# Layer 0's recurrence: GpSimd makes both tiles' gating products and the query products beside VectorE's four sums, and the first stage is put in another order

## The reference, cut to what matters

```python
def step(carry, xs):                       # 32 chunks, one after the other
    W_in, W_out = carry                    # each 4 x 8 per sequence and head
    q_t, k_t, v_t, lr_t = xs
    k_h = softmax(einsum('blhd,bDhd->blhD', k_t, W_in), -1) * lr_t[..., 1:]
    q_h = softmax(einsum('blhd,bDhd->blhD', q_t, W_in), -1)
    qk = einsum('bqhD,bkhD->bhqk', q_h, k_h) * mask
    o_t = einsum('bqhD,bDhd->bqhd', q_h, W_out) + einsum('bhqk,bkhd->bqhd', qk, v_t)
    W_out = W_out + einsum('bnhD,bnhd->bDhd', k_h, v_t)
    for _ in range(2):
        g_out, g_in = -attn(W_in, k_t, v_t), -attn(W_out, v_t, k_t)
        W_in, W_out = W_in - lr_in * g_in, W_out - lr_out * g_out
    return (W_in, W_out), o_t
...
# the experts: top 2 of 8 for each token
gate = silu(x @ wg.T); up = x @ wu.T; y = (gate * up) @ wd.T
```

## Time and profile before

| | |
|---|---|
| median of 3 runs | 1335.31 us |
| the profiled execution | 1332.25 us |
| its span, first to last instruction | 1330.5 us |
| VectorE busy | 1224.0 us (92%) |
| TensorE busy | 1002.1 us (75%), mean granted clock 0.873 |
| ScalarE busy | 718.4 us (54%) |
| GpSimd busy | 701.5 us (53%) |
| step 0 of the recurrence begins | 126.07 us |
| step 4, the first with experts, begins | 203.92 us |
| step 28 begins | 646.56 us |
| the last step, 31, begins | 710.05 us |

### The profile page before, as it was taken

One profiled execution on the slowest core, in us unless ns is written; L12 is line 12 of the kernel. 1 busy time (PEld: TensorE's weight loads), 2 busy tenths in 40 slices (PEclk: granted clock), 3 DMA queues, 4 the chain that ended last, 5 costly groups with the idle time before them and its releaser, 6 DMA issues. The chain is left out here.

```text
span 1330.5 us, 15940 instructions
## 1 busy us (share of the span) xinstructions
PE 1002.1 (75%) x3654; PEld 580.4 (44%) x3655; DVE 1224.0 (92%) x2277; ACT 718.4 (54%) x1364; POOL 701.5 (53%) x637
## 2 busy tenths in 40 slices
PE   3865347878878887787577576668899889898874
PEld 2522335555555555555445532233444444444431
DVE  7998799999999999999997779989999899989999
ACT  5654015555555555555334565457667666766741
POOL 5038732333333333333210017789789778878885
PEclk9687558889889889999877598789999899999988
DMA  9749141000000000000162124455445444543346
GB/s 304 217 115 310 58 134 41 21 20 22 21 24 18 24 16 21 24 18 18 52 204 64 32 103 129 143 141 176 159 152 182 162 140 172 163 156 139 137 150 191
DMA packets 106772, 145.49 MB, mean 109 GB/s; under 512 B 26348, under 2 KB 82425, under 8 KB 101857
## 3 DMA queue, kind: packets, MB, share of 16 engines
q1 hardware_dynamic: 90816, 114.51, 27.2%
q0 software_dynamic: 10240, 25.32, 5.9%
q10 hardware_dynamic: 5664, 5.11, 1.2%
HBM read 112.26 MB, written 39.04 MB: 114 GB/s over the span
## 5 line engine op out<-in xcount | busy, mean ns | idle before, releaser
L2126 DVE TENSOR_TENSOR ps<-ps,cv 128x512 f32<-128x512 f32 x256 | 162.4, 679 | 1.9 <-DMA cv<-bc_scr 1.9
L1160 PE MATMUL ps<-Q,ident 128*128 128x512 f32 x206 | 115.2, 649 | 24.2 <-DVE Q L2144 7.5
L985 PE MATMUL ps<-wd_a,xn 128*128 x576 | 93.9, 313 | 42.8 <-ACT xn L1374 42.8
L1392 ACT ACTIVATE x<-x 128x128 f32<-128x128 f32 (+1 forms) x127 | 32.2, 278 | 143.3 <-DVE x L1953 65.0
L782 POOL DMA_INDIRECT y_tok<-xnT,meta x72 | 72.7, 1010 | 61.6 <-ACT xnT L1380 48.9
L965 PE MATMUL ps<-wg_a,xnT 128*128 x144 | 90.9, 717 | 17.5 <-issue 11.2
L985 PEld LDWEIGHTS ps<-wd_a,xn 128*128 128x128 f32 x576 | 79.2, 213 | 56.8 <-issue 55.3
L995 PE MATMUL ps<-x,ident 128*128 128x64 f32 x512 | 73.7, 297 | 29.1 <-DMA wu_a<-in_wu_a 12.3
L760 POOL DMA_INDIRECT slots_x<-xn,sl_put x64 | 75.2, 1174 | 37.9 <-issue 18.9
L791 POOL TENSOR_TENSOR xn<-xn 128x512 f32<-128x512 f32 x24 | 30.3, 1264 | 120.7 <-DVE x L1947 111.0
L995 PEld LDWEIGHTS ps<-x,ident 128*128 128x128 f32 x512 | 73.0, 217 | 43.4 <-issue 33.4
(11 more groups left out here) (383 smaller groups left out, 3041.0 us busy)
## 6 DMA issues: line engine op xcount, KB each, us to landing
cv<-bc_scr SPq DMA_DIRECT2D x64, 512.0 KB
xn<-bc_scr SPq DMA_DIRECT2D x24, 1024.0 KB
O<-bc_scr SPq DMA_DIRECT2D x8, 1024.0 KB
slots_x<-O POOLq DMA_DIRECT2D x28, 260.0 KB, 5.6
qkv_scr<-wg_a SPq DMA_DIRECT2D x24, 256.0 KB
xnT<-slots_x SPq DMA_DIRECT2D x72, 64.0 KB
x<-in_x SPq DMA_DIRECT2D x8, 512.0 KB, 6.4
y_tok<-slots_x SPq DMA_DIRECT2D x2, 2048.0 KB, 13.8
```

Source lines behind the costliest of these rows:

```text
L985: m = pe.matmul(ps[:, 0, 0:D], hidT[:, k, f * P:(f + 1) * P], wd_a[:, bass.ds(off + f * D, D)], start=(f == 0), stop=(f == FC - 1))
L1160: pe.matmul(ps[:, 4, :], ident[:], yc_of(c, n), start=(n == 0), stop=(n == NS - 1)).then_inc(y0_used, 1)
L2126: tt(dBu(g), ps[:, 2 + g, :], b_rows[:, n % 4, :], ALU.mult).then_inc((inject0, b_used)[g], 1)
```

## The change

In the recurrence: GpSimd also makes the gating product of tile 1 (ScalarE copies its up product first), beside L1963; tile 0's stays beside L1949; the step's own query product now goes beside L1894, the output product beside L1978. VectorE keeps only tile 2's. TensorE makes `o_sums` at the end of a routed step. One semaphore, `sum_begins`, counts the first two large products of each step. In the first stage: the query norms go ahead of the last four value projections and start with each square; ScalarE squares the queries ahead of the values' silus; the second half of V is loaded in two pieces; the gate copies are spread around the learning rates; the gate projections use seven banks, so that they need not wait for copies; TensorE waits for the experts' weights in step 3 and not before step 0.

```diff
@@ heads_load: rows lo to hi, and SyncE's calls
-            heads_load(sp, 1, 2, V, v_in)
+            heads_load(sp, 4, 6, 2, V, v_in)
+            heads_load(sp, 6, 8, 2, V, v_in)
@@ GpSimd
             def q_product(c):
-                pool.wait_ge(p3_ready, c)
+                pool.wait_ge(sum_begins, 2 * c + 1)
                 pool.wait_ge(q_ps, c)
                 pq_of(pool, c).then_inc(pq_ready, 1)
             def o_product(c):
                 pool.wait_ge(qh_ready, c + 1)
                 pool.wait_ge(o_ps, c + 1)
+                pool.wait_ge(p3_ready, c + 1)
                 op_of(pool).then_inc(op_ready, 1)
-            q_product(FIRST)
...
-            def gated_first(c):
-                pool.wait_ge(gate_silu, (c - FIRST) * TPS + 1)
-                pool.wait_ge(up_copied, c - FIRST + 1)
-                pool.wait_ge(p2_ready, c + 1)
-                pool.tensor_tensor(hid[:, 0, :], th[:, 0, :], up0, ALU.mult).then_inc(hid0_ready, 1)
+            def gated(c, k):
+                pool.wait_ge(gate_silu, (c - FIRST) * TPS + k + 1)
+                pool.wait_ge(up_copied, (c - FIRST) * (TPS - 1) + k + 1)
+                if k:
+                    pool.wait_ge(qh_ready, c + 1)
+                else:
+                    pool.wait_ge(sum_begins, 2 * c + 2)
+                pool.tensor_tensor(hid[:, k, :], th[:, k, :], ups[:, k, :], ALU.mult).then_inc(hid_pool, 1)
             for c in range(FIRST, NCH - 1):
+                q_product(c)
+                if FIRST < c <= AFTER:
+                    y_scatter(c - 1, 1)
                 if c < AFTER:
-                    gated_first(c)
+                    gated(c, 0)
                 if FIRST < c <= AFTER:
-                    y_scatter(c - 1, TPS - 1)
+                    y_scatter(c - 1, 2)
+                if c < AFTER:
+                    gated(c, 1)
+                    y_scatter(c, 0)
                 o_product(c)
-                q_product(c + 1)
-                if c < AFTER:
-                    for k in range(TPS - 1):
-                        y_scatter(c, k)
+            q_product(NCH - 1)
@@ TensorE
             def norms(n, sq, bank):
-                pe.wait_ge(squared, 4 * n + 4)
                 for e in range(HD):
+                    if e % 2 == 0:
+                        pe.wait_ge(squared, 4 * n + e // 2 + 1)
...
+            pe.wait_ge(lr_copied, B)
+            norms(1, sq_q, 7)
             for b in range(4, B):
                 project(2 * B + b)
-            pe.wait_ge(lr_copied, B)
-            norms(1, sq_q, 7)
             for b in range(B):
                 pe.wait_ge(conv_done, NCU)
-                since(pe, gate_copied, b - 3)
+                if b == 4:
+                    pe.wait_ge(slots_ready, 1)
+                since(pe, gate_copied, b - 6)
...
-            pe.wait_ge(slots_ready, 1)
-            pe.wait_ge(we_loaded, 16 * 3)
@@ TensorE, step
                 q_sums(c, 4, HD)
+                if after and not here:
+                    o_sums(c)
                 for k in range(2):
...
-                    if k == 0:
+                    if k == 0 and not here and not after:
                         o_sums(c)
+                if here:
+                    o_sums(c)
             with pe.Fori(0, FIRST - 1) as c:
                 step(c, False)
+            pe.wait_ge(slots_ready, 1)
+            pe.wait_ge(we_loaded, 16 * 3)
@@ ScalarE
+            act.wait_ge(q_in, 32)
+            for k in range(4):
+                square(Q, sq_q, 2 * k)
+            silu(2 * B)
+            for b in range(1, B):
                 silu(2 * B + b)
-                if b < 4:
-                    tap(2 * B + b + 4)
-...
+                if b < 5:
+                    tap(2 * B + b + 3)
             act.preload_act_table(ACT.Sqrt)
             norm_roots(1, 7)
...
             act.preload_act_table(ACT.Exp)
+            act.wait_ge(lr_stored, 16)
+            for b in range(3):
+                gate(b)
             act.wait_ge(lr_in, 1)
...
+            for b in range(3, B - 1):
+                gate(b)
             act.preload_act_table(ACT.Exp)
-            act.wait_ge(v_in, 32)
+            gate(B - 1)
@@ ScalarE, step
-                if not start:
-                    o_copy(c - 1)
                 if before:
                     y(c - 1, 1)
                 if here:
                     xT(c, 2)
+                if not start:
+                    o_copy(c - 1)
                 if before:
                     hT(c - 1, 2)
+                if start:
+                    act.wait_ge(v_in, 48)
...
                 if here:
+                    up_copy(c, 1)
                     act.preload_act_table(ACT.Silu)
...
-                if after:
+                if after and here:
                     xT(c + 1, 0)
                 exp(EQ, rec_q, exp_q)
...
                 if here:
                     y(c, 0)
+                if after and not here:
+                    xT(c + 1, 0)
                 if after:
-                    up_copy(c + 1)
+                    up_copy(c + 1, 0)
                     xT(c + 1, 1)
@@ VectorE, step
-                tt(PP, bc(VC, 1, 2 * DI), bc(both(WO[:]), 2, CH), ALU.mult).then_inc(p2_ready, 1)
-                dve.wait_ge(p2_ready, c + 1)
+                tt(PP, bc(VC, 1, 2 * DI), bc(both(WO[:]), 2, CH), ALU.mult).then_inc(sum_begins, 1)
+                dve.wait_ge(sum_begins, c * 2 + 2)
...
                 q_softmax()
-                gated(1)
                 if late:
```

More of the change, by code:

```diff
@@ L201, in build, with gate_bank @@
         logit_bank, rank_bank = (0, 1), (1, 2)
+        def gate_bank(b):
+            return (2, 3, 4, 5, 0, 1, 6)[b % 7]
         ring = wg_a[:].rearrange("p (u t) -> p u t", t=L)
@@ L210, in build @@
         r = Region(xn_rows[:])
-        th, hid, up0 = r.take(TPS, F), r.take(TPS, F), r.take(F)
+        th, hid, ups = r.take(TPS, F), r.take(TPS, F), r.take(TPS - 1, F)
         hidT = th
@@ L548, in op_of, with heads_load @@
             return eng.tensor_tensor(OP, bc(EQ, 2, HD), CS.rearrange("p (D e) l -> p D e l", D=DI)[:, :, :, 1:CH + 1], ALU.mult)
-        def heads_load(eng, half, w, dst, done):
-            turn = 2 * (1, 0, 2).index(w) + half
-            for u in range(4):
-                eng.wait_ge(stored[4 * (turn % 2) + u], 16 * (turn // 2 + 1))
-            eng.dma_start(dst[half * 64:(half + 1) * 64, :, :],
-                          qkv_scr[w, 4 * half:4 * half + 4].rearrange("b (h e) t -> (b h) e t", h=H)).then_inc(done, 16)
+        def heads_load(eng, lo, hi, w, dst, done):
+            for b in range(lo, hi):
+                eng.wait_ge(stored[b], 16 * ((1, 0, 2).index(w) + 1))
+            eng.dma_start(dst[lo * H:hi * H, :, :],
+                          qkv_scr[w, lo:hi].rearrange("b (h e) t -> (b h) e t", h=H)).then_inc(done, 16)
         block = ctx.enter_context(nc.Block())
@@ L742, in _ @@
                                pad).then_inc(zeroed, 16)
[L744 to L747 removed]
+            heads_load(pool, 0, 4, 1, K, k_in)
+            heads_load(pool, 4, 8, 1, K, k_in)
+            heads_load(pool, 0, 4, 0, Q, q_in)
+            heads_load(pool, 4, 8, 0, Q, q_in)
             pool.wait_ge(zeroed, ZEROED)
@@ L1332, in _, with gate @@
                 lr_copy(b)
-            for b in range(B):
-                silu(2 * B + b)
-                if b < 4:
-                    tap(2 * B + b + 4)
-                k = b - 2
-                if 0 <= k < 4:
-                    if k == 0:
-                        act.wait_ge(q_in, 32)
-                    square(Q, sq_q, 2 * k)
+            act.wait_ge(q_in, 32)
[3 more added lines that the diff above has]
+            for b in range(1, B):
+                silu(2 * B + b)
+                if b < 5:
+                    tap(2 * B + b + 3)
             act.preload_act_table(ACT.Sqrt)
             norm_roots(1, 7)
+            def gate(b):
+                act.wait_ge(gate_ps, b + 1)
+                act.activation(gateT[:, b * L:(b + 1) * L], ps[:, gate_bank(b), :], ACT.Copy).then_inc(gate_copied, 1)
             act.preload_act_table(ACT.Exp)
+            act.wait_ge(lr_stored, 16)
+            for b in range(3):
+                gate(b)
             act.wait_ge(lr_in, 1)
@@ L1349, in _ @@
             act.activation(LR[:], LR[:], ACT.Ln, bias=1.0).then_inc(lr_log, 1)
-            act.wait_ge(lr_stored, 16)
-            for b in range(B):
-                act.wait_ge(gate_ps, b + 1)
-                act.activation(gateT[:, b * L:(b + 1) * L], ps[:, 2 + b % 4, :], ACT.Copy).then_inc(gate_copied, 1)
+            for b in range(3, B - 1):
+                gate(b)
             act.preload_act_table(ACT.Exp)
-            act.wait_ge(v_in, 32)
+            gate(B - 1)
             temper = HD ** -0.5
@@ L1892, in step @@
                 r_k = o.mark(dve.reciprocal(Z3K[:, j:], Z3K[:, j:]))
-                o.wait(g_3)
+                dve.wait_ge(sum_begins, c * 2 + 1)
```

(6 more changed lines are left out.)

31 lines of the change are left out of this document (14 added, 17 removed).

## The result

| | before | after |
|---|---|---|
| median of the first measurement, 10 runs each | 1335.2 us | 1330.6 us |
| ratio, 95% interval | | 0.9956 [0.9938, 0.9975] |
| the profiled execution | 1332.25 us | 1329.91 us |
| its span | 1330.5 us | 1328.2 us |
| step 0 begins | 126.07 | 118.30 |

The forecast was 1322.6 us in a range of 1313.0 to 1330.0. The kernel became faster, by 4.6 us where 12.7 were expected, and its median lies 0.6 us above the range. The last two rows say where to look: layer 0 is 11.2 us shorter, close to the forecast, and layer 1, whose code is the same, took 8.8 us longer.

A forecast was written before the change was run, and what follows sets the result against it. VectorE, busy 92% of the span, was taken to bound the kernel. The terms -11.7 + 2.3 + 2.5 - 15.1 + 6 + 3.3 = -12.7 us gave a median of 1322.6 us, range 1313.0 to 1330.0.

The forecast's parts named there:

- first stage to step 3: First stage of layer 0: VectorE's waits of 3.27, 2.64 and 5.75 us go, -11.7 us.
- step 3 into 4: Step 3 of layer 0: output sums ahead of the first tile's transpose make step 4 begin at 194.5, +2.3 us.
- tiles of steps 4, 5: Steps 4 and 5: the fourth tile's rows come late behind the clearings, +2.5 us, bounds 0 and 5.
- routed steps: 24 routed steps: without tile 1's product VectorE saves 0.63 us a step, -15.1 us.
- late steps: Routed steps behind stretches of lower clock: ScalarE comes late in 6 or 7 of them, 0.9 us each, +6 us.
- tail: End of layer 0: output products 3.3 us later delay TensorE's variance sums, +3.3 us, bounds 0.5 and 4.5.
- further on everything follows VectorE: Behind the last steps of layer 0: everything keeps pace with VectorE, no further gain or loss, 0 us.
- the rival of the lock: Routed steps: VectorE's L1967 waits 0.26 us each for GpSimd's product, 6.2 us in all, result 1328.8 us; chance 0.13.
- VectorE stays the only bound: Layer 0: ScalarE's reserve holds, the clock's falls go, the tiles are hidden: -25 us, 1310 us; chance 0.14.
- ScalarE's stream: Each routed step: ScalarE's work becomes the bound and VectorE waits for it, +13.7 us, 1349 us, slower; chance 0.06.

The follow-up runs named there:

- e13: The changed kernel with GpSimd making only 384 of the 512 columns of tile 1's gating product: 1319.1 us, ratio 0.9871 to the kernel before.
- e9: The changed kernel with GpSimd's output product and tile 1's gating product in each other's place: 1398.9 us, ratio 1.0453 to the kernel before.
- e8: The changed kernel with one unused TensorE matmul of 512 columns in each routed step: 1318.4 us, ratio 0.9877 to the kernel before.
- e4: The changed kernel's new recurrence order with the first stage as before: 1337.3 us, ratio 0.9992 to the kernel before.
- e10: The changed kernel with the 4 MB of clearings spread in eight pieces behind the fourth to eleventh tile's loads: 1323.7 us, ratio 0.9908 to the kernel before.
- e2: The kernel before, unedited, run again for a second profile: 1339.9 us, ratio 1.0011 to the kernel before.
- e7: The kernel before with two unused TensorE matmuls filling a pause in each row of layer 1: 1331.4 us, ratio 0.9973 to the kernel before.

## Why the prediction was wrong

Against the first profiles, term by term (us, forecast and measured):

| term | forecast | measured | from |
|---|---|---|---|
| first stage to step 3 | -11.7 | -13.5 | 185.79 to 172.26 |
| step 3 into 4 | +2.3 | +1.7 | 19.78 - 18.13 |
| tiles of steps 4, 5 | +2.5 | +3.5 | 19.85 + 19.59 - 2 x 17.97 |
| routed steps | -15.1 | -11.3 | 24 x (18.44 - 17.97) |
| late steps | +6 | +4.4 | steps 6 to 27, 399.72 - 22 x 17.97 |
| tail | +3.3 | +4.2 | -15.36 to -11.17 |
| layer 0 | -12.7 | -11.2 | |
| "further on everything follows VectorE" | 0 | +8.8 | 629.3 - 620.4 |

- **The step that failed** is the last sentence of the tail. I did not look into layer 1, since the change does not touch it. But its time is no constant: in all 17 profiles the rest took 617 to 629 us, and most of that hangs on whether TensorE's clock falls after pauses that are always there (rows 2 to 6, 315 to 326 us). With the rest of before, the profiled execution would have come at 1321.1 us. The sum had no term for this spread, and it is about as large as the whole forecast. The first profile of before (13.6 us of low clock in rows 2 to 6) was one of the short sort, that of after (27.2 us) one of the long.
- **The routed steps' term** was mis-sized. The 0.63 us did go, but each L1991 lost 0.14 to GpSimd's product (one of them 0.45), 3.6 us in 24. That is the rival of the lock, whose place was right and whose price (0.26 us each, 6.2 us) was too high: I took the overlap for the loss, but an instruction of 0.22 us whose end waits for a product with 0.28 us to go ends only 0.14 later. (From the earlier trace rows the overlap comes to 568.10 - 567.91 = 0.19 us, not the 0.26 written.) The row that I set against it showed an overlap of 0.11 us, too short to delay anything. The Trainium skill (SBUF — State Buffer, Terms) speaks of a lock held for the full instruction; e13 and L1977 in e9 agree with it.
- **The first stage** gave more than forecast, all three waits whole and a fourth. **Late steps**: seven, each 0.3 to 0.7 us, of the 6 or 7 at 0.9 forecast; the mechanism was right (e8). **The tail**: a wait of about 3 us before L2030 was forecast and 2.97 came; 1.5 us were missed in step 28, where VectorE's L1972 waits 2.21 us for ScalarE. The query sums of the last step came 0.81 us late, where the forecast had 0.3; this lies behind the start of step 31. **Step 3 and the tiles**: the mechanisms right (e4, e10), the sizes 0.6 us less and 1.0 more.
- **Luck.** That layer 0 as a whole came within 1.5 us of its forecast is in part luck: the first stage, step 3 and the late steps came out 4.0 us better than forecast, the routed steps, the tiles and the tail 5.7 us worse.
- The rival "VectorE stays the only bound" fell with the late steps, that of ScalarE's stream did not come about; e9 shows how near it is.
- **The measurement.** On two other chips the unedited change gained 0.8 to 0.9%, 11 to 12 us, about layer 0's gain and close to the forecast; the first measurement's 4.6 us came from runs of which seven lay at 1329.9 to 1333.0 us and three at 1325.1 to 1327.1. On the other two chips most runs lay in the lower heap (four of six, four of five). Why the first measurement drew the long sort so often with the changed kernel and the short with the one before is open; the runs show only that both kernels can have either. The first profile of before was also its best in the first stage: the wait before L1916 was 5.75 us there and 8.7 to 9.6 in the three later profiles with the old first stage (e2, e4, e7), where step 3 began at 187.1 to 188.1. The change removes this wait whatever its length. VectorE in e2:

```profile
142.07 0.22 DVE L1916 TENSOR_REDUCE MQ<-ps 128x16 f32<-128x64 f32 x1 [8.83 <-PE ps L995]
```

## What to carry to other kernels

A stage that an edit does not touch still has to be looked at when its start moves: where it has pauses behind which the clock sometimes falls and sometimes doesn't, its time is a spread, and one profile of each kernel compares two draws. Compare stage by stage, with two or three profiles each, before a difference is put down to the change. A pause of TensorE that decides over the clock can be filled with matmuls for nobody as long as they are shorter than the pause; and work moved beside a sum must end before the next instruction with two tensor operands does, or that one pays inside its own duration, where no wait shows.

## What the runs showed of the hardware

- Matmuls that nobody uses can make a kernel faster (0.27% in e7): one of 512 columns in each routed step took the lower clock out of the 360 us of both windows of e8 (PEclk 1.00) and its steps' late 0.6 us with it.
- VectorE's product of two tensors is held while GpSimd's product runs, inside its recorded time: 0.36 us instead of 0.22 with 0.28 us of overlap, 0.67 when GpSimd's ran 0.59 us into it, 1.37 instead of 0.31 under a whole product. In the clean and late steps L1991 ended 0.08 to 0.09 us after GpSimd's product, whatever the overlap. The large sum beside the same product, which reads one tensor, kept its 1.21 us, and a small one (L2004) its 0.29 with up to 1.05 us of a product still to run.

The changed kernel's step 8, GpSimd and VectorE:

```profile
279.16 1.21 DVE L1987 TENSOR_REDUCE GR<-cv 128x64 f32<-128x1024 f32 x1
279.74 1.26 POOL L797 TENSOR_TENSOR xn<-xn 128x512 f32<-128x512 f32 x1 [2.37 <-DVE x L1954]
280.41 0.67 DVE L1991 TENSOR_TENSOR GR<-GR,Z2Q 128x64 f32<-128x64 f32 x1
```

- Moving one product 3.4 us later cost 73 us from step 6 to step 28 (e9), 3.3 in each of 22 steps: nearly its whole delay, since the tile chain of silu, transpose, down and the next gate and up closes into a ring.
